# The chunk of the maximum pass ahead of the scores, in TensorE's queue and in the ring of PSUM banks

## The chip, the cores and the metric

The kernel runs on one core of one Trainium2 chip. The metric is the time of one execution in microseconds (us) of device time. Engines: TensorE multiplies matrices (PE in the profile, PEld for its weight loads), VectorE is DVE, ScalarE is ACT, GpSimd is POOL, SyncE is SP and issues DMAs.

## The reference

A block with cross attention and a mixture of experts, float32, for a batch of 4, 256 queries and 1601 keys, model width 128, 16 heads of 8:

```python
x = x + tanh(g_xattn[0]) * xattn(layernorm(x), ctx, ctx, mask, W_Q, W_K, W_V, W_T)
x = x + tanh(g_ffn[0]) * ffn(layernorm(x), w1, w2, router_w)
# xattn: heads of 8 columns
score = einsum('bhqd,bhkd->bhqk', Q, K) / sqrt(8)
score = where(mask == 0, -1e9, score)
out = einsum('bhqk,bhkd->bhqd', softmax(score), V) @ W_T
# ffn: 8 experts of 256, the two best by router
h = einsum('td,eid->tei', x, w1)
y = h[..., 256:] * silu(h[..., :256])
out = einsum('tei,ehi,te->th', y, w2, combine)
```

## The kernel before

The work is cut into 16 units, one for each of 4 batches and 4 groups of 4 heads; unit u is group u % 4 of batch u // 4. For an exact softmax each row of scores needs its maximum first. So TensorE computes the scores twice: once with queries in the rows, in chunks of up to 512 keys, of which VectorE takes the maximum (the maximum pass, 26 chunks a unit, `chunk`, L1013 and L757), and once with keys in the rows (`scores`, L1031), where the negated maximum is already in, as three more rows of the queries. ScalarE takes the exponential of these (`exponentials`, L622), and TensorE multiplies them by the values (`probs_v`, L1064).

A unit has 26 slots. In each slot stands one scores item, two key tiles of 128 keys for one head, a bank full; and one chunk. The chunks run 12 slots ahead of the scores (`LEAD`), so most are of the next unit; in the first 24 slots of unit 0 every even slot has two, until the lead is reached. `chunks_in(n)` lists the chunks of slot n. There are none after slot 13 of unit 14. A chunk of 512 keys is one matmul; chunks 12 and 25 of a unit hold the last 65 keys of four heads, in four short matmuls.

Both kinds of item go through one ring of five PSUM banks. `ring_tables` (L132) deals the banks out in the order of TensorE's queue, and notes for each item which item had its bank before; `ring_free` (L1008) makes TensorE wait until that one has been read, by ScalarE (`probs_ready`) for scores or by VectorE (`chunk_used`) for a chunk.

All engines run through the units and slots in the same written order, each with its own queue. After scores and chunk, a slot can have on TensorE:

- a piece of the key or value projection for a later batch (`piece`, L1050), in units 0 to 3;
- values times exponentials: four key tiles at once in slots 9, 17 and 25 (32 matmuls with those of two passes), the last short tile in slot 2 of the next unit;
- the transposes of the finished heads (slot 8) and of the negated maxima of the next unit (slot 17, L953; slot 20 in unit 0);
- in the first unit of each batch from the second on, for the batch before: slot 12 transposes the heads, slot 14 projects them (L1125), slot 20 transposes the normalised rows (L1131), slot 22 computes the router (L1136);
- in the other three units of such a batch, for the batch before: a tile of an expert's first layer every 4 or 5 slots (`expert_up`, L1100; slots 3, 8, 12, 16, 21, 25 of unit 6), and an expert's second layer six slots after its second tile (`expert_down`, L1108; slots 5, 14, 22 of unit 6).

VectorE's queue has in each slot the chunk's maximum (L767) first, then what the slot has for it: the gating of a tile (L853, L857), which waits for ScalarE's tanh (L659) of that tile; the add of an expert (L865); in a first unit the residual and statistics (slot 14, L797 to L804), the norm (slot 18, L811), the two best experts (slot 22, L819 to L828); in a second unit the routing weights (slot 1, L834 to L843). ScalarE's queue has the exponential first, then the rest.

At slot 0 of a unit the scores wait for the negated maxima's rows (`neg_in`), which a DMA has brought. The first chunk of a unit waits for that unit's keys and queries (`ld_unit`). Unit 0 starts 43.5 us after the span's start, unit 2 at 99.5, unit 4 at 149.3, unit 5 at 170.4, unit 6 at 198.8, unit 7 at 225.4, unit 8 at 250.4, unit 14 at 401.0 and unit 15 at 422.8 us.

Of the kernel before, what the change touches and what calls it, by code (L numbers as in the profile page):

```python
# [101 lines left out]
def following(b, q, by=1):  # L102

    return (b + (q + by) // NQ, (q + by) % NQ)


def chunk_rows(n):

    t, r = divmod(n, QH * (CH - 1) + 1)
    if r < QH * (CH - 1):  # L110
        return t, [r % QH], r // QH
    return t, list(range(QH)), CH - 1


def chunk_at(g):

    return 1 + g // CHUNKS, g % CHUNKS


def chunks_in(n):  # L120

    first = n + min(LEAD, (n + 1) // 2)
    last = n + 1 + min(LEAD, (n + 2) // 2)
    return [g for g in range(first, last) if g < CHUNKS * (B * NQ - 1)]


def neg_slot(u, s):

    return s + (FIRST_LATER if u == 0 else 0)


def ring_tables():  # L132

    banks, before = {}, {}
    latest = {i: ("quad", len(QUADS)) for i in range(RING)}
    item = 0
    for n in range(B * NQ * SLOTS):
        for kind, m in [("scores", n)] + [("chunk", g) for g in chunks_in(n)]:
            bank = item % RING
            banks[kind, m] = bank  # L140
            before[kind, m] = latest[bank]
            latest[bank] = (kind, m + 1)
            item = item + 1
    return banks, before


def piece_at(slot):

    u, s = divmod(slot, SLOTS)
    if s not in PIECE_SLOTS or u < 0:  # L150
        return None
    n = u * len(PIECE_SLOTS) + PIECE_SLOTS.index(s)
    return n if n < len(PIECES) else None
# [12 lines left out]
def expert_work(b, q, s, after=0):  # L166

    return [n for n, at in enumerate(TILE_AT[b - 1]) if at + after == (q - 1) * SLOTS + s]
# [7 lines left out]
def value_tiles(s):  # L176

    at = [VISIT // 2 * QH * (t // VISIT + 1) + 1 for t in range(KT - 1)] + [SLOTS + 2]
    return [(at[t] // SLOTS, t) for t in range(KT) if at[t] % SLOTS == s]


def block_kernel(nc, x, ctxT, mask, g_x, g_f, W_Q, W_K, W_V, W_T, w1T, w2T, rT, out):
# [5 lines left out]
    with es:  # L188
# [81 lines left out]
        ring, pv_bank, up_bank, down_bank = bank[0:RING], bank[5], bank[6], bank[7]  # L270
        down_b = down_bank.bitcast(BF16)
        ring_bank, ring_before = ring_tables()


# [645 lines left out]
        def _(pe):  # L920
# [84 lines left out]
            def attention(with_mask):  # L1005


                def ring_free(kind, n):  # L1008

                    earlier, count = ring_before[kind, n]  # L1010
                    pe.wait_ge({"scores": probs_ready, "chunk": chunk_used, "quad": quad_used}[earlier], count)

                def chunk(g):  # L1013

                    u, n = chunk_at(g)
                    q = u % NQ
                    if n == 0:
                        pe.wait_ge(ld_unit[q], 16 * (PARTS + 1) * (u // NQ + 1))

                    t, heads_in, c = chunk_rows(n)  # L1020
                    dst = ring[ring_bank["chunk", g]]
                    ring_free("chunk", g)
                    for i, j in enumerate(heads_in):
                        last = nc.tensor.matmul(dst[:, i * CW[c]:(i + 1) * CW[c]], queries[q][0:ROWS, j, t * P:(t + 1) * P],  # L1024
                                                keys[q][0:ROWS, j, c * BANK:c * BANK + CW[c]], start=True, stop=not with_mask)
                        if with_mask:
                            last = nc.tensor.matmul(dst[:, i * CW[c]:(i + 1) * CW[c]], ident_neg[:, :],
                                                    masked_q[:, t, c * BANK:c * BANK + CW[c]], start=False, stop=True)
                    last.then_inc(chunk_ready, 1)

                def scores(b, q, s):  # L1031

                    if s == 0:
                        pe.wait_ge(neg_in, 16 * PARTS * (NQ * b + q + 1))
                    n = SLOTS * (NQ * b + q) + s
                    slot_bank = ring[ring_bank["scores", n]]
                    ring_free("scores", n)
                    for i in range(2):
                        j, t = (s % QH, 2 * (s // QH) + i) if s < QH * (STEPS - 1) else (2 * (s % QH) + i, KT - 1)
                        w = P if t < KT - 1 else TAIL  # L1040
                        dst = slot_bank[0:w, i * S:(i + 1) * S]
                        last = nc.tensor.matmul(dst, keys[q][0:KR, j, t * P:t * P + w], queries[q][0:KR, j, :],  # L1042
                                                start=True, stop=not with_mask)
                        if with_mask:
                            for half in range(QT):
                                last = nc.tensor.matmul(dst[:, half * P:(half + 1) * P], masked_q[:, half, t * P:t * P + w],
                                                        ident_neg[:, :], start=False, stop=half == QT - 1)
                    last.then_inc(scores_ready, 1)

                def piece(n):  # L1050

                    kind, b, i = PIECES[n]
                    hold(pe, piece_out, n)
                    if b and (n == 0 or PIECES[n - 1][1] != b):
                        pe.wait_ge(ld_ctx[b], 16)
                    if kind == "Q":
                        cols = slice(S + i * BANK, min(S + (i + 1) * BANK, B * S))
                        made = nc.tensor.matmul(up_bank[:, 0:cols.stop - cols.start], wq[:, :], xnT[:, cols],
                                                start=True, stop=True)
                    else:  # L1060
                        made = project_keys(b, i, up_bank) if kind == "K" else project_values(b, i, up_bank)
                    made.then_inc(piece_ready, 1)
# [85 lines left out]
                def units(b, tail, attn, last):  # L1148
                    for q in range(NQ):
                        u = NQ * b + q  # L1150
                        for s in range(SLOTS):
                            before = not (q == 0 and not tail) and (attn or q == 0)
                            if attn:
                                scores(b, q, s)
                                for g in chunks_in(SLOTS * u + s):
                                    chunk(g)
                                if piece_at(SLOTS * u + s) is not None:
                                    piece(piece_at(SLOTS * u + s))
                            for back, kt in value_tiles(s):
                                if before if back else attn:  # L1160
                                    probs_v(u - back, (q - back) % NQ, kt)
                            if s == S_OTR and before:
                                pe.wait_ge(out_copied, u)
                                down_bank_free(b, tail, q, s, attn, last)
                                for t in range(QT):
                                    tr = nc.tensor.transpose(down_bank[:, t * P:(t + 1) * P],
                                                             head_outT[:, t * P:(t + 1) * P], ident[:, :])
                                tr.then_inc(out_T, 1)
                            if s == neg_slot(u, S_MTR) and attn and not (last and q == NQ - 1):
                                down_bank_free(b, tail, q, s, attn, last)  # L1170
                                neg_transpose(*following(b, q))
                            if tail and q == 0:
                                if s in (S_PROJ, S_ROUTE):
                                    down_bank_free(b, tail, q, s, attn, last)
                                tail_slot(b, s)
                            for n in expert_work(b, q, s) if tail and attn else ():
                                expert_up(b, n, [up_bank])
                            for n in expert_work(b, q, s, DOWN_AFTER) if tail and attn else ():
                                if n % TILES == TILES - 1:
                                    down_bank_free(b, tail, q, s, attn, last)  # L1180
                                    expert_down(b, n // TILES, down_bank)
                            if q == 0 and not attn:
                                fill_slot(b, s)
# [62 lines left out]
```

## Time and profile before

| what | value |
|---|---|
| time, median of 3 runs | 481.47 us (477.12 to 485.35) |
| profiled execution: its own time | 480.24 us |
| profiled execution: span | 478.4 us |
| granted TensorE clock, mean | 0.978 |
| TensorE busy | 444.4 us, 93% |
| VectorE busy | 350.6 us, 73% |
| ScalarE busy | 273.9 us, 57% |
| GpSimd busy | 85.9 us, 18% |

The span goes from the first to the last instruction; the execution's time has some 2 us around it. Busy times are of one execution. The ends of matmuls are modelled, and neighbouring ones overlap in the rows, so the distance of two starts tells more than a duration.

### The profile page before, as it was taken

How to read it: one execution, taken by the hardware profiler on the slowest of the kernel's cores; microseconds unless marked ns; L12 is line 12 of the kernel's file. 1: busy time of each engine (PE TensorE's matmuls, PEld its weight loads, DVE VectorE, ACT ScalarE, POOL GpSimd, SP SyncE). 2: the span in 40 equal slices, each digit the busy share in tenths (PEclk: the TensorE clock that was granted, in tenths of full speed). 3: DMA queues.
4: the chain of work that ended last, by engine and by line, in shares of the span. 5: the costliest groups of instructions: out<-in, count | busy, mean ns of one | idle time of the engine just before them, and what ended most of it. 6: DMA issues, size and time to landing. Idle time of an engine off the chain costs nothing.

```text
span 478.4 us, 10091 instructions
## 1 busy us (share of the span) xinstructions
PE 444.4 (93%) x3864; PEld 266.6 (56%) x3866; DVE 350.6 (73%) x768; ACT 273.9 (57%) x569; POOL 85.9 (18%) x207
## 2 busy tenths in 40 slices
PE   7873999998999999999999999999999989999896
PEld 3331555644554556666665556666655456566786
DVE  3971786764768897887888987888879777531786
ACT  4201666764768665665657665665667565687221
POOL 4800508236820100000001100000001000000000
PEclk9995999999999999999999999999999898999999
DMA  7476626693734040404014403012052200000000
GB/s 271 99 166 170 141 79 159 185 241 107 194 106 103 5 87 0 91 3 87 6 35 80 88 6 78 14 43 50 2 113 46 46 2 1 2 13 1 1 11 12
DMA packets 20701, 35.23 MB, mean 74 GB/s; under 512 B 2236, under 2 KB 12924, under 8 KB 20524
## 3 DMA queue, kind: packets, MB, share of 16 engines
q1 hardware_dynamic: 19348, 33.96, 29.5%
q10 hardware_dynamic: 1304, 0.59, 0.5%
q8 instruction: 33, 0.54, 0.5%
q14 instruction: 16, 0.13, 0.1%
HBM read 26.49 MB, written 7.80 MB: 72 GB/s over the span
## 4 chain that ended last, share of the span: by engine, by line
PE 69%; DVE 14%; ACT 5%; DMA 4%; issue 4%; POOL 2%; SPq 0%; POOLq 0%; DVEq 0%; ACTq 0%
PE banks L1076 19%; PE banks L1042 16%; PE banks L1024 13%; PE banks L1100 10%; PE banks L1108 5%; DVE chunk_max L767 5%; DMA queries<-neg_rows 3%; DVE chunk_max L749 3%; ACT probs L636 3%; PE banks L931 2%; DVE late L853 2%; PE banks L925 1%; DVE late L857 1%; DMA probs<-x 1%; ACT late L659 1%
## 5 line engine op out<-in xcount | busy, mean ns | idle before, releaser
L767 DVE TENSOR_REDUCE chunk_max<-banks 128x1 f32<-128x512 f32 (+1 forms) x390 | 240.0, 663 | 67.4 <-PE banks L1024 66.6
L636 ACT ACTIVATE probs<-banks 128x512 f32<-128x512 f32 x384 | 210.8, 605 | 94.6 <-PE banks L1042 93.7
L1042 PE MATMUL banks<-queries,keys 75*128 75x256 bf16 (+1 forms) x832 | 157.0, 276 | 13.9 <-DMA queries<-neg_rows 9.2
L1024 PE MATMUL banks<-keys,queries 72*128 72x512 bf16 x480 | 146.7, 339 | 2.2 <-DVE chunk_max L767 0.9
L1042 PEld LDWEIGHTS banks<-queries,keys 75*128 75x128 bf16 (+1 forms) x832 | 72.0, 100 | 82.9 <-DVE chunk_max L767 28.9
L1076 PE MATMUL banks<-probs,value_t 128*9 128x256 f32 x1536 | 93.6, 384 | 0.1
L1076 PEld LDWEIGHTS banks<-probs,value_t 128*9 128x9 f32 x1536 | 37.4, 91 | 46.3 <-issue 12.1
L1024 PEld LDWEIGHTS banks<-keys,queries 72*128 72x128 bf16 x480 | 42.3, 97 | 22.5 <-ACT probs L636 7.6
L659 ACT ACTIVATE late<-banks 128x256 f32<-128x256 f32 x64 | 24.6, 385 | 49.6 <-PE banks L1100 44.1
L853 DVE SCALAR_TENSOR_TENSOR late<-late,banks 128x256 f32<-128x256 f32 x64 | 26.7, 417 | 30.1 <-ACT late L659 30.0
L1100 PE MATMUL banks<-xn2T,w 128*128 128x256 f32 x128 | 35.4, 400 | 1.3 <-DVE late L857 1.3
L1108 PE MATMUL banks<-w,late 128*128 128x128 f32 x256 | 34.0, 276 | 1.2 <-DVE late L857 1.0
L1108 PEld LDWEIGHTS banks<-w,late 128*128 128x128 f32 x256 | 33.1, 191 | 3.1 <-DVE x L865 1.2
L1100 PE MATMUL banks<-late,w 128*128 128x256 f32 x128 | 32.0, 381 | 0.0
L469 POOL COPY value_t<-values 128x384 f32<-128x384 f32 x16 | 8.0, 503 | 130.7 <-PE banks L1076 127.7
L530 POOL TENSOR_SCALAR neg_max<-row_max 128x8 f32<-128x8 f32 x16 | 3.8, 236 | 145.2 <-DVE row_max L744 145.2
L857 DVE TENSOR_TENSOR late<-late,banks 128x256 f32<-128x256 f32 x64 | 26.9, 421 | 2.2
L1100 PEld LDWEIGHTS banks<-xn2T,w 128*128 128x128 f32 x128 | 24.1, 199 | 6.2 <-DVE late L857 2.1
L865 DVE SCALAR_TENSOR_TENSOR x<-banks,combine,x 128x128 f32<-128x128 f32 x64 | 19.3, 343 | 8.8 <-PE banks L1108 8.7
L1100 PEld LDWEIGHTS banks<-late,w 128*128 128x128 f32 x128 | 23.2, 190 | 3.7 <-issue 0.9
L645 ACT COPY neg_rows<-banks 12x256 bf16<-12x256 bf16 x16 | 5.8, 360 | 27.8 <-PE banks L953 27.8
L639 ACT ACTIVATE probs_tail<-banks 65x512 f32<-65x512 f32 x32 | 17.6, 591 | 1.6 <-PE banks L1042 1.6
(121 smaller groups left out, 288.2 us busy)
## 6 DMA issues: line engine op xcount, KB each, us to landing
keys<-k_parts SPq DMA_DIRECT2D x48, 300.2 KB
k_parts<-split SPq DMA_DIRECT2D x6, 400.2 KB, 7.6
ctx_in<-ctxT SPq DMA_DIRECT2D x3, 800.5 KB, 5.2
k_parts<-late SPq DMA_DIRECT2D x6, 400.2 KB, 4.8
queries<-q_parts SPq DMA_DIRECT2D x16, 144.0 KB
w<-w1T SPq DMA_DIRECT2D x1, 2048.0 KB, 14.8
q_parts<-q_split SPq DMA_DIRECT2D x9, 192.0 KB, 2.6
w<-mask SPq DMA_DIRECT2D x2, 800.5 KB, 6.6
```

The source lines that it names most:

```text
L636: nc.scalar.activation(probs[:, s % (HELD * QH), :], ring[ring_bank["scores", n]][:, :], ACT.Exp, scale=SCALE).then_inc(probs_ready, 1)
L639: nc.scalar.activation(probs_tail[0:TAIL, s % QH, :], ring[ring_bank["scores", n]][0:TAIL, :], ACT.Exp, scale=SCALE).then_inc(probs_ready, 1)
L659: nc.scalar.activation(th[:, n % 2, :], bank[:, 0:S], ACT.Tanh, scale=0.5).then_inc(th_ready, 1)
L767: nc.vector.reduce_max(dst, src, axis=AX.X).then_inc(chunk_used, 1)
L853: steps.link(nc.vector.scalar_tensor_tensor(gated[:, :], th[:, n % 2, :], 1.0, bank[:, 0:S], ALU.add, ALU.mult))
L857: nc.vector.tensor_tensor(inner[:, n % 4, :], gated[:, :], bank[:, S:2 * S], ALU.mult).then_inc(inner_ready, 1)
L865: last = nc.vector.scalar_tensor_tensor(x1[:, t, :], bank[:, t * D:(t + 1) * D], combine[:, t, e:e + 1], x1[:, t, :], ALU.mult, ALU.add)
L1024: last = nc.tensor.matmul(dst[:, i * CW[c]:(i + 1) * CW[c]], queries[q][0:ROWS, j, t * P:(t + 1) * P], keys[q][0:ROWS, j, c * BANK:c * BAN ...
L1042: last = nc.tensor.matmul(dst, keys[q][0:KR, j, t * P:t * P + w], queries[q][0:KR, j, :], start=True, stop=not with_mask)
L1076: last = nc.tensor.matmul(pv_bank[32 * j:32 * j + HW, 0:S], value_t[q % 2][0:w, kt, j, :], p, start=kt == 0, stop=kt == KT - 1)
L1100: last = nc.tensor.matmul(banks[n % len(banks)][:, k * S:(k + 1) * S], w1[:, e, k * INTER + i * P:k * INTER + (i + 1) * P], xn2Ts[b % 2][: ...
L1108: last = nc.tensor.matmul(bank[:, t * D:(t + 1) * D], inner[:, (TILES * e + i) % 4, t * P:(t + 1) * P], w2[:, e, i, :], start=i == 0, stop ...
```

## The change

In the loop of TensorE's queue the call of `scores` moves from ahead of the slot's chunks to behind them. `ring_tables` gives out the banks in the same new order. VectorE's, ScalarE's and the other queues stay as they are.

```diff
--- before.py
+++ after.py
@@ -135,7 +135,7 @@
     latest = {i: ("quad", len(QUADS)) for i in range(RING)}
     item = 0
     for n in range(B * NQ * SLOTS):
-        for kind, m in [("scores", n)] + [("chunk", g) for g in chunks_in(n)]:
+        for kind, m in [("chunk", g) for g in chunks_in(n)] + [("scores", n)]:
             bank = item % RING
             banks[kind, m] = bank
             before[kind, m] = latest[bank]
@@ -1151,9 +1151,9 @@
                         for s in range(SLOTS):
                             before = not (q == 0 and not tail) and (attn or q == 0)
                             if attn:
-                                scores(b, q, s)
                                 for g in chunks_in(SLOTS * u + s):
                                     chunk(g)
+                                scores(b, q, s)
                                 if piece_at(SLOTS * u + s) is not None:
                                     piece(piece_at(SLOTS * u + s))
                             for back, kt in value_tiles(s):
```

## Rows read from the trace of the kernel before

**Rows 1.** The page: TensorE's busy time; the chain's shares by engine.

```profile
PE 444.4 (93%) x3864; PEld 266.6 (56%) x3866; DVE 350.6 (73%) x768; ACT 273.9 (57%) x569; POOL 85.9 (18%) x207
...
PE 69%; DVE 14%; ACT 5%; DMA 4%; issue 4%; POOL 2%; SPq 0%; POOLq 0%; DVEq 0%; ACTq 0%
```

**Rows 2.** Windows: units 4 and 6; length, each engine's busy us, clock.

```profile
149.30:170.40 21.10, 20.26 (x208) 11.34 (x204) 18.20 (x45) 14.74 (x30) 2.63 (x9) 1.00 0.30 58
198.80:225.40 26.60, 26.49 (x242) 17.23 (x240) 22.16 (x47) 16.25 (x34) 1.67 (x7) 1.00 0.21 43
```

**Rows 3.** Waits: who waited for whom, us in all, times, longest.

```profile
PEld banks L1042 <- DVE chunk_max L767: 28.9, 78, 1.2
...
PE banks L1042 <- DMA queries<-neg_rows: 9.2, 2, 8.2
...
PEld banks L1024 <- ACT probs L636: 7.6, 29, 0.6
```

**Rows 4.** Groups by form: busy us and mean ns of one.

```profile
L767 DVE TENSOR_REDUCE chunk_max<-banks 128x1 f32<-128x512 f32 x360 | 228.3, 683 | 56.0 <-PE banks L1024 55.3 <-DVE combine L843 0.3
L636 ACT ACTIVATE probs<-banks 128x512 f32<-128x512 f32 x384 | 210.8, 605 | 94.6 <-PE banks L1042 93.7
```

**Rows 5.** The chain, slots 0 to 9 of unit 7: start, us, what.

```profile
225.64 0.22 PE banks L1042 x2
225.86 0.12 PE banks L1024 x4
...
226.99 0.55 PE banks L1076 x8
...
228.09 0.86 PE banks L1100 x4
...
229.61 0.22 PE banks L1024
229.83 0.89 PE banks L1108 x8
...
233.53 0.22 PE banks L1042 x2
...
233.97 1.84 PE banks L1076 x32
```

**Rows 6.** Timeline, unit 7: start, us, engine, line, count of merged instructions.

```profile
226.89 2.21 DVE L767 TENSOR_REDUCE chunk_max<-banks 128x4 f32<-128x260 f32 x4
227.48 0.39 PE L1042 MATMUL banks<-queries,keys 75*128 75x256 bf16 x2
230.20 1.28 DVE L767 TENSOR_REDUCE chunk_max<-banks 128x1 f32<-128x512 f32 x2
231.54 0.28 PE L1042 MATMUL banks<-queries,keys 75*128 75x256 bf16 x1
...
231.91 1.88 DVE L767 TENSOR_REDUCE chunk_max<-banks 128x1 f32<-128x512 f32 x3
...
235.97 0.38 PE L1024 MATMUL banks<-keys,queries 72*128 72x512 bf16 x1
...
236.39 0.69 DVE L767 TENSOR_REDUCE chunk_max<-banks 128x1 f32<-128x512 f32 x1 [0.85 <-PE banks L1024]
```

**Rows 7.** Timeline, slots 17 and 25 of unit 4, and VectorE there.

```profile
161.28 0.38 PE L1042 MATMUL banks<-queries,keys 75*128 75x256 bf16 x2
...
161.81 0.66 DVE L767 TENSOR_REDUCE chunk_max<-banks 128x1 f32<-128x512 f32 x1
...
168.05 0.40 PE L1042 MATMUL banks<-queries,keys 75*65 75x256 bf16 x2
...
169.09 3.05 DVE L767 TENSOR_REDUCE chunk_max<-banks 128x1 f32<-128x512 f32 x5
```

**Rows 8.** Windows: 3.4 us of unit 5, and the 3.4 us after them.

```profile
173.80:177.20 3.40, 2.59 (x15) 1.00 (x14) 3.37 (x7) 2.57 (x5) 0.00 (x0) 1.00 0.11 20
177.20:180.60 3.40, 3.40 (x12) 2.08 (x9) 2.05 (x6) 1.21 (x3) 0.00 (x0) 0.50 0.02 5
```

## The prediction, as it was made before the result

> **What bounds the kernel now.** I read first which engine is full, then by units what is full where, then whose waits are met, and only then single instructions. The page gives TensorE 93% of the span, and the chain of waits puts 69% of it on TensorE and 14% on VectorE [rows 1]. By stretches, the units with expert work (unit 6, 26.6 us) have TensorE busy 26.49 us, so nearly every us added to its queue is a us of the span; VectorE is busy 22.16 us there, 83%. In unit 4 (a first unit of a batch) TensorE has 20.26 of 21.10 us [rows 2]. TensorE is the bound from unit 4 on, with VectorE close behind. In the list of waits TensorE's weight loads wait 28.9 us for VectorE's maxima in front of scores and 7.6 us for ScalarE's exponentials in front of chunks [rows 3]. Most of this is covered, since loads run ahead of matmuls: the chain through unit 7 is TensorE alone, 28 of its 29 pieces, of which rows 5 has the eight that I use [rows 5]. So ring waits cost almost nothing now, though many are nearly due. The question is which of them come due earlier.
>
> **The change, part by part.** No instruction is added or removed; every slot still has one scores item, its chunks and then its rest (value tiles, an expert tile, a transpose). What moves:
>
> 1. *The banks.* Five banks go round, scores and chunks in turn. Before, item 2n is the scores of slot n, and the item five back is the chunk of slot n-3; the chunk's is the scores of slot n-2. After, the scores need the bank of the chunk of slot **n-2**, and the chunk that of the scores of slot **n-3**. TensorE may enter the rest of a slot before with three chunks unread by VectorE and two scores unread by ScalarE, afterwards with two chunks and three scores. The buffer is moved from the slower reader to the faster one: a chunk takes VectorE 683 ns, a scores tile takes ScalarE 605 ns, and VectorE alone also has the gating and adding for the experts [rows 4]. Unit 0, where even slots have two chunks, is different: five items to two slots, each bank is taken again by its own kind two slots later in both orders, so nothing changes there.
>
> 2. *The queue.* The chunk goes 0.22 us earlier and the scores 0.22 us later (length of one chunk, 0.12 for the one of four short matmuls) [rows 5]. TensorE's total is the same, so this alone costs zero. At a unit's first slot the chunk passes the wait for the row of negated maxima; the list has 9.2 us of that in two places [rows 3], which a chunk can't shorten; it fills 0.22 us of it each time, and a little of VectorE's work. I take -0.4 us for both. A chunk that waited for keys would now hold the scores behind it; no row shows TensorE waiting for keys, so zero.
>
> 3. *Waits on ScalarE.* At least one slot more lies between exponential and chunk. That can save what now stands on ScalarE, between 0 and the 7.6 us of weight load waits [rows 3]. I count it where it shows: the places of before that I subtract below hold those waits, the places of after don't.
>
> 4. *Waits on VectorE.* This is the term that decides, and I work it out slot by slot for unit 7 with rows' durations. Scores 0.22, chunk 0.22 (0.12 in slots 0 and 13), short value tile 0.55, expert tile up 0.86, down 0.89, visit to the values 1.84 [rows 5]. VectorE starts a chunk 0.42 after its matmul starts (235.97 to 236.39), needs 0.68, back to back 0.59 to 0.60 each (five in 3.05 [rows 7]), and the bank can be written 0.06 after the end (two chunks from 230.20 on end at 231.48, the scores start at 231.54). After an expert tile the next chunk starts 1.41 after the tile's last matmul (225.48 to 226.89), since VectorE's in-order queue waits at the gate for ScalarE's tanh; an add of an expert costs it 0.51 (the second of those two chunks starts at 230.80, the next at 231.91; less 0.60) [rows 6].
>
> Clock zero at 225.48, the end of the tile at the previous slot 25. Chunk 0 starts at 0, scores 0 at 0.12, chunk 1 at 0.35, scores 1 at 0.57, chunk 2 at 0.79, scores 2 would start at 1.01. It needs chunk 0, which VectorE reads from 1.41 to 1.83: **wait of 0.88**. In the order before, it is the scores of slot 3 that need chunk 0, and they start at 227.48, 0.16 us after that read's end [rows 6]. Then the short value tile, chunk 3 and scores 3 (2.99), the tile up to 4.08. Chunks 4 and 5, down, chunk 6: scores 6 wait 0.15 for chunk 4, scores 7 wait 0.16 for chunk 5, scores 8 wait 0.67 for chunk 6, which stands behind the add. The tile of slot 8 ends at 9.54; before, this was 7.89 (from 225.64 to 233.53 on the chain [rows 5]). **Slots 0 to 9: +1.65.** In slots 10 to 17 scores 12 wait 0.05 and scores 16 wait 0.37 (chunk 14 behind the gate): **+0.44**. In slots 18 to 25 of unit 6, scores 20, 21 and 24 wait 0.05, 0.16 and 0.16, and scores 25 wait 0.67 for chunk 23, which stands behind an add: with what was waited there before taken off, **+0.97**; in unit 7, with no tile at 21, +0.5.
>
> First units of a batch (4, 8, 12) have no expert tiles, but three VectorE jobs that wait for TensorE. Slots 3 to 9: +0.16. Scores of slot 17 need chunk 15, which stands behind the residual and is read from 161.81 to 162.47, where TensorE was at slot 17 at 161.28: with the short delays before it (0.39 at the projection, whose exponentials come 0.22 later) +1.44. Scores of slot 25 need chunk 23, behind the top-2 search and read from 169.09 to 169.77, where TensorE was at 168.05 [rows 7]: with the scores' own place 0.22 later and the norm's 0.22 earlier, +1.57. About **+3.1** a unit. Second units (5, 9, 13): scores 4 need chunk 2 behind the routing weights, a little over 1 us, but there TensorE waited before too: +0.8 in slots 0 to 9.
>
> Sum: slots 0 to 9 of units 6, 7, 10, 11, 4 x 1.65 = 6.6; slots 10 to 17 of six units, 2.6; slots 18 to 25, 4 x 0.97 + 2 x 0.5 = 4.9; first units 3 x 3.1 = 9.3; second units 3 x 0.8 = 2.4; the rest of 13 and 14, where tiles are rarer and which I only estimate, 1.5; units 1 to 3, where the same working gives gains at ScalarE waits (slots 5 to 9 of unit 2, -0.2) and losses of the same size, 0; unit starts -0.4. Together **+26.9 us**. From unit 14's middle on there are no chunks, so nothing. Ends of this term: if readers catch up in ways that the working misses, half of it, +13; if every unit from 1 to 14 lost the 3.1 of the dearest kind, +43.
>
> 5. *TensorE's clock.* In one stretch of 3.4 us in unit 5 the granted clock is 0.50, that is 1.2 instead of 2.4 GHz, and in the 3.4 us before it TensorE was busy for 2.59 us only [rows 8]; two more stretches like it are in unit 13. Each costs half its length, 1.7 us. The same pattern in unit 9 passed without it, so it isn't certain. The new waits of 0.65 us or more make some 24 such stretches (waits as in slots 2, 8, 25, 17) where there were some seven, of which three were throttled. At that rate seven more; since several have less idle time than the old ones I take three more, **+5 us**; ends 0 and 24 x 1.7 = 41.
>
> The Trainium skill ("TensorE: Matmul & The Clock Gate", "A second HAM failure mode: psum-queue depth-cycling") says that short idle times between matmul groups which cycle through PSUM banks can make the clock swing between its two rates. The trace before shows three swings and agrees as far as it goes; taken fully the rule gives the first rival below, by which the sum would be nearer its upper end.
>
> Profiled execution 480.24 us (span 478.4, 1.8 us around it) + 26.9 + 5 = 512.1; it lies 1.2 us under the median of 481.47, so I say **512 us**.
>
> **The rivals.**
> *The clock swings all through*: mechanism of step 5 at its upper end. For it: three of the seven idle stretches of before were followed by it; against: the other four. 480 + 27 + 30 to 41 us = 537 to 548.
> *VectorE catches up*: it has 17% free in unit 6, and a wait of TensorE gives it time. If a delayed scores item only moves idle time that now comes later at the values' visit, the loss is a few us: 480 + 5 = 485. Against: TensorE has no idle time in unit 6 to give back (26.49 of 26.6).
> *Faster*: ScalarE's waits go (7.6 us of loads [rows 3]) and the chunk passes the wait for the negated maxima. Place: units 1 to 3, which have no expert work, and the starts of units 0 and 2. At best 7.6 + 2 x 0.7 (a chunk less to read after the wait) = 9 us: 471. It decides if chunk n-2 is read by the time scores n come, that is if VectorE's backlog stays under two chunks; the gate rows say that it doesn't.
> That the change doesn't act is excluded by the bank table.
>
> **How the numbers follow.** Forecast 0.76 (its own range 496 to 530); clock rival 0.08; catching up 0.12; faster 0.04. No change means within 2%, 9.6 us, about what this kernel's measurements (477.12 to 485.35) can tell. Faster by over 2% is half of the last case, 0.02; within 2% is the other half, and catching up, 0.14; slower 0.84. The range reaches to the lower end of the clock rival and, at the bottom, to half of step 4's sum: 494 to 538; outside are the two lowest cases, 0.16, and some of the clock rival.
>
> **What would show it.** In the changed profile: scores matmuls idle before them on chunk_max, tens of us in place of a few, with waits of 0.7 to 1.1 us in slots 2, 8 and 25; chunks no longer waiting for ScalarE; unit 6 at 29.7 us and unit 4 at 24.2 us; units 0 to 3 within 0.5 us each; from slot 14 of unit 14 the same length; more clock rows at 0.50. The forecast is wrong if VectorE's waits at gates shrink because the tiles move against its queue, which my working holds fixed at 1.41 us.

## The result, and the profile after

The changed kernel takes 511.18 us (median of 4 executions, 504.75 to 520.44) beside 479.64 us before (477.12 to 485.35): a ratio of 1.065 with a 95% interval of 1.059 to 1.072, slower. Forecast were 512 us and a range of 494 to 538. An execution's time moves with its mean granted clock: of the four of the changed kernel the shortest had 0.978, the longest 0.949. The profiled execution took 510.16 us, its span is 508.4 us.

Of the page: TensorE's busy line, the granted clock in 40 slices, the chain's shares, and the group of the scores matmuls (busy us, mean ns | idle time before them, and what ended it).

```profile
PE 459.7 (90%) x3864; PEld 259.5 (51%) x3866; DVE 352.4 (69%) x768; ACT 284.2 (56%) x569; POOL 86.0 (17%) x207
...
PEclk9995699999999989999999999999999799999999
...
PE 60%; DVE 20%; ACT 6%; issue 5%; DMA 4%; POOL 3%; ACTq 1%; SPq 0%; POOLq 0%; DVEq 0%
...
L1042 PE MATMUL banks<-queries,keys 75*128 75x256 bf16 (+1 forms) x832 | 160.9, 280 | 22.1 <-DVE chunk_max L767 21.8
```

Against [rows 1] the instructions are the same in number, and VectorE's work has hardly grown, yet its share of the chain went from 14% to 20% and TensorE's from 69% to 60%. The list of waits (us in all, times, longest) has the place, and answers to [rows 3]:

```profile
PEld banks L1042 <- DVE chunk_max L767: 69.1, 141, 1.5
...
PE banks L1042 <- DVE chunk_max L767: 21.8, 36, 1.1
...
PE banks L1024 <- DMA queries<-q_parts: 7.7, 1, 7.7
...
PEld banks L1024 <- ACT probs L636: 5.8, 17, 0.4
```

Weight loads of scores wait 69.1 us for VectorE's maxima instead of 28.9, and the matmuls themselves 21.8 us in 36 places. The same row for the matmuls in the kernel before:

```profile
PE banks L1042 <- DVE chunk_max L767: 4.3, 7, 0.8
```

Slots 0 to 9 of unit 7 in the changed kernel, the stretch that the prediction replayed, in the timeline of TensorE (start, us, engine, line; a scores item is one row of two matmuls):

```profile
238.41 0.28 PE L1024 MATMUL banks<-keys,queries 72*128 72x65 bf16 x4
...
239.19 0.38 PE L1024 MATMUL banks<-keys,queries 72*128 72x512 bf16 x1
240.30 0.39 PE L1042 MATMUL banks<-queries,keys 75*128 75x256 bf16 x2 [0.73 <-DVE chunk_max L767]
240.62 0.62 PE L1076 MATMUL banks<-probs_tail,value_t 65*9 65x256 f32 x8
241.18 0.39 PE L1024 MATMUL banks<-keys,queries 72*128 72x512 bf16 x1
...
244.26 0.38 PE L1024 MATMUL banks<-keys,queries 72*128 72x512 bf16 x1
244.64 0.39 PE L1042 MATMUL banks<-queries,keys 75*128 75x256 bf16 x2
...
245.24 0.39 PE L1042 MATMUL banks<-queries,keys 75*128 75x256 bf16 x2
245.47 0.38 PE L1024 MATMUL banks<-keys,queries 72*128 72x512 bf16 x1
246.35 0.39 PE L1042 MATMUL banks<-queries,keys 75*128 75x256 bf16 x2 [0.50 <-DVE chunk_max L767]
246.58 0.40 PE L1166 MATMUL banks<-ident,head_outT 128*128 128x128 f32 x2
246.81 1.03 PE L1100 MATMUL banks<-xn2T,w 128*128 128x256 f32 x4
247.68 0.38 PE L1024 MATMUL banks<-keys,queries 72*128 72x512 bf16 x1
```

And VectorE there (the row at 239.82 is three chunks merged, of which chunk 0 is the first):

```profile
239.03 0.42 DVE L853 SCALAR_TENSOR_TENSOR late<-late,banks 128x256 f32<-128x256 f32 x1 [2.63 <-ACT late L659]
239.48 0.42 DVE L857 TENSOR_TENSOR late<-late,banks 128x256 f32<-128x256 f32 x1
239.82 1.61 DVE L767 TENSOR_REDUCE chunk_max<-banks 128x4 f32<-128x260 f32 x3
...
245.10 0.60 DVE L865 SCALAR_TENSOR_TENSOR x<-banks,combine,x 128x128 f32<-128x128 f32 x2
```

With clock zero at 238.41, the scores of slot 2 start at 1.89; they could have at 1.00 (239.19 and 0.22). What they wait for is chunk 0, at the head of VectorE's row at 239.82 and behind the two gating instructions; ahead of the first VectorE sat idle for 2.63 us until tanh came. Scores 6, 7 and 8 start at 6.23, 6.83 and 7.94, the last 0.66 late behind the add at 245.10. The waits of the prediction, added up from the same zero, put them at 1.89, 6.23, 6.83 and 7.94.

In the chain of the changed kernel, answering to [rows 5], what was TensorE alone is now a relay of ScalarE, VectorE and TensorE:

```profile
238.61 0.39 ACT late L659
...
239.03 0.43 DVE late L853
...
239.48 0.42 DVE late L857
239.90 0.35 DVE chunk_max L767
240.25 0.05 issue
240.30 0.39 PE banks L1042 x2
```

The lengths of the units (start of a unit's first scores to the next unit's, from the timeline), before, after, and in a second profile of the changed kernel (run e12 below), with what was forecast:

| unit | before | after | again | difference, e12 to before | forecast |
|---|---|---|---|---|---|
| 0 | 30.47 | 34.74 | 30.34 | -0.1 | within 0.5 |
| 4 | 21.15 | 25.21 | 25.46 | 4.3 | 3.1 |
| 6 | 26.61 | 29.46 | 29.47 | 2.9 | 3.1 |
| 7 | 24.94 | 27.40 | 27.40 | 2.5 | 2.6 |
| 8 | 21.16 | 23.83 | 23.83 | 2.7 | 3.1 |
| 9 | 26.74 | 28.92 | 28.94 | 2.2 | 2.2 |
| 12 | 21.16 | 25.07 | 23.84 | 2.7 | 3.1 |
| 4 to 14 | 273.47 | 298.86 | 298.65 | 25.2 | 27.3 |

Unit 4 holds a stretch of 3.4 us with the clock at 0.50 in both profiles of the changed kernel and none in that of before; without it its loss is that of unit 8. Over units 4 to 14 the profile of before and that of e12 have three such stretches each, so the 25.2 us are nearly all the banks'.

### The profile page after: what moved, and what is told of

Its sections match the earlier page's. It is cut to its first block, busy times and chain, and to the rows that moved or that the text cites. A ratio compares the mean times of both kernels' runs of the same rounds, so it can differ in the third digit from the quotient of the medians.

```text
span 508.4 us, 10091 instructions
## 1 busy us (share of the span) xinstructions
PE 459.7 (90%) x3864; PEld 259.5 (51%) x3866; DVE 352.4 (69%) x768; ACT 284.2 (56%) x569; POOL 86.0 (17%) x207
## 4 chain that ended last, share of the span: by engine, by line
PE 60%; DVE 20%; ACT 6%; issue 5%; DMA 4%; POOL 3%; ACTq 1%; SPq 0%; POOLq 0%; DVEq 0%
PE banks L1076 19%; PE banks L1042 14%; DVE chunk_max L767 10%; PE banks L1024 10%; PE banks L1100 9%; DVE late L853 3%; ACT late L659 2%; PE banks L1108 2%; ACT probs L636 2%; PE banks L925 2%; DMA queries<-q_parts 2%; PE banks L931 2%; DVE x L865 2%; DVE late L857 2%; ACTq L608 1%
## 5 line engine op out<-in xcount | busy, mean ns | idle before, releaser
L636 ACT ACTIVATE probs<-banks 128x512 f32<-128x512 f32 x384 | 215.4, 604 | 118.7 <-PE banks L1042 116.7
L1042 PE MATMUL banks<-queries,keys 75*128 75x256 bf16 (+1 forms) x832 | 160.9, 280 | 22.1 <-DVE chunk_max L767 21.8
L1024 PE MATMUL banks<-keys,queries 72*128 72x512 bf16 x480 | 149.5, 346 | 8.6 <-DMA queries<-q_parts 7.7
L1042 PEld LDWEIGHTS banks<-queries,keys 75*128 75x128 bf16 (+1 forms) x832 | 70.8, 101 | 108.5 <-DVE chunk_max L767 69.1
L1076 PE MATMUL banks<-probs,value_t 128*9 128x256 f32 x1536 | 95.8, 390 | 0.1
L853 DVE SCALAR_TENSOR_TENSOR late<-late,banks 128x256 f32<-128x256 f32 x64 | 26.8, 418 | 43.9 <-ACT late L659 43.5
L1108 PEld LDWEIGHTS banks<-w,late 128*128 128x128 f32 x256 | 31.6, 191 | 2.7 <-DVE x L865 1.2
L857 DVE TENSOR_TENSOR late<-late,banks 128x256 f32<-128x256 f32 x64 | 26.9, 420 | 2.2
L1100 PEld LDWEIGHTS banks<-xn2T,w 128*128 128x128 f32 x128 | 22.7, 197 | 5.7 <-DVE late L857 2.1
L639 ACT ACTIVATE probs_tail<-banks 65x512 f32<-65x512 f32 x32 | 18.8, 594 | 7.5 <-PE banks L1042 7.3
```

The costliest lines, as they stand in the source:

```text
L636: nc.scalar.activation(probs[:, s % (HELD * QH), :], ring[ring_bank["scores", n]][:, :], ACT.Exp, scale=SCALE).then_inc(probs_ready, 1)
L639: nc.scalar.activation(probs_tail[0:TAIL, s % QH, :], ring[ring_bank["scores", n]][0:TAIL, :], ACT.Exp, scale=SCALE).then_inc(probs_ready, 1)
L853: steps.link(nc.vector.scalar_tensor_tensor(gated[:, :], th[:, n % 2, :], 1.0, bank[:, 0:S], ALU.add, ALU.mult))
L857: nc.vector.tensor_tensor(inner[:, n % 4, :], gated[:, :], bank[:, S:2 * S], ALU.mult).then_inc(inner_ready, 1)
L1076: last = nc.tensor.matmul(pv_bank[32 * j:32 * j + HW, 0:S], value_t[q % 2][0:w, kt, j, :], p, start=kt == 0, stop=kt == KT - 1)
L1100: last = nc.tensor.matmul(banks[n % len(banks)][:, k * S:(k + 1) * S], w1[:, e, k * INTER + i * P:k * INTER + (i + 1) * P], xn2Ts[b % 2][: ...
```

## The experiments

All run beside the kernel before on the same chip: its median was 481.33 us beside e1 to e4, 483.58 beside e5 to e8 and 478.75 beside e9 to e12. An execution's clock moves its time by up to 4%, so for differences smaller than that the units' lengths decide, which agree to 0.02 us between two profiles of one kernel except where the clock was at 0.50.

**Where the loss lies: units from 4 on, units to 3 (e4, e5).** The new order in both places, for part of the slots (`ring_tables` has the same condition, not shown here):

```diff
+scores_first = not ((SLOTS * u + s) >= 4 * SLOTS)      # e5: not (... < 4 * SLOTS)
+if scores_first:
+    scores(b, q, s)
 for g in chunks_in(SLOTS * u + s):
     chunk(g)
-scores(b, q, s)
+if not scores_first:
+    scores(b, q, s)
```

> The change from unit 4 on only; units 0 to 3 as before. Theory: units 4 to 14 carry the whole of it, +25 us without clock stretches: 503 to 512 us, unit 6 at 29.5 us, units 0 to 3 at their old lengths. Rival (unit 0's +4.2 us in the changed kernel belongs to the new order there, through the clock): this one is 4 us faster than the changed kernel, and its unit 0 has the clock at 0.50 for 10 us after 37 us, not 20.

> The change in units 0 to 3 only. Theory: 480 us, the same as before within 3; unit 0's +4.2 us in the changed kernel came from TensorE's clock, which stayed at 0.50 for 20 us after 39.6 us there by the chance of one execution. Rival (the new order at the start of unit 0 keeps the clock low): +4 us and again some 20 us at 0.50.

e4: 513.2 us (505.56 to 519.75), ratio 1.064 (1.047 to 1.081), 1 us over the 503 to 512 expected; units 6 and 7 at 29.47 and 27.40 us, as in the changed kernel. e5: 481.96 us beside 483.58, units 4 to 12 as before within 0.01 us but for unit 5, which escaped a clock stretch (26.74 for 28.41). So units 4 to 14 carry all of it, within what the clock lets be seen. Unit 0 with the new order took 30.42 us in e5: its 34.74 us in the changed kernel's first profile isn't the order's. There the clock was at 0.50 for 20.5 us from 39.6 on, in e5 for 10.2 us from 38.3 on.

**Once more the same (e12).** No edit.

> The changed kernel once more, for what varies between executions. Theory: the waits on VectorE are the same to 0.1 us in each unit (unit 6 29.5, unit 7 27.4 us), the stretches with the clock at 0.50 lie elsewhere and unit 0's is 10 us long in most executions; 503 to 513 us. Rival: unit 0 has 20 us at 0.50 again.

505.58 us (505.12 to 506.77), ratio 1.058 (1.051 to 1.064). Unit lengths as in the table: only units with a clock stretch in one of the two profiles, or in both, differ. The 10 us in unit 0 came as expected.

**The two halves of the diff (e1, e2).** e1 has only the edit in TensorE's queue, e2 only the one in `ring_tables`.

> The queue of the change with the banks of before: TensorE issues chunk, then scores, but the scores of slot n still take the bank of chunk n-3 and the chunk that of scores n-2. Theory (VectorE lost one of its three unread chunks ahead of a slot's rest): nothing is lost, 480 us, give or take 4; unit 6 stays at 26.6 us. Rival (the place in the queue costs: exponentials come 0.22 us later, so tanh and gates come later): most of the +31 us stays, 505 to 515 us.

> The banks of the change with the queue of before: TensorE issues scores, then chunk, and the scores of slot n take the bank of chunk n-2. Theory: all the loss is there and more, since the scores reach that wait one chunk (0.22 us) earlier and hold the slot's own chunk behind them: 515 to 540 us. Rival (queue order): 480 us.

e1: 503.28 us (496.02 to 515.89), ratio 1.045 (1.031 to 1.058). Unit 6 took 28.16 us, unit 4 23.60. The theory was wrong, and the rival's number (505 to 515) nearly met, but the waits of e1 say something that neither had:

```profile
PEld banks L1024 <- ACT probs L636: 53.4, 128, 0.6
...
PE banks L1024 <- ACT probs L636: 20.1, 83, 0.4
...
PEld banks L1042 <- DVE chunk_max L767: 4.8, 15, 0.4
```

VectorE is waited for by almost nothing, as the theory has it, but chunks wait for ScalarE 83 times. With the banks of before and the queue of the change a chunk is only three items behind the scores whose bank it takes, 0.66 us in slots without a rest, and a scores item needs over 1 us from its start to the end of its exponential, here from 213.97 to 214.99 (timeline of e1):

```profile
213.97 0.38 PE L1042 MATMUL banks<-queries,keys 75*128 75x256 bf16 x2
...
214.39 0.60 ACT L636 ACTIVATE probs<-banks 128x512 f32<-128x512 f32 x1
```

e2 is the mirror (`PEld banks L1042` waits for VectorE again, here in e2): 548.92 us (543.53 to 553.28), ratio 1.141 (1.128 to 1.154), unit 6 at 31.22 us; scores are three items behind the chunk whose bank they take, and wait 97 times for VectorE:

```profile
PEld banks L1042 <- DVE chunk_max L767: 108.1, 170, 1.7
PE banks L1042 <- DVE chunk_max L767: 44.9, 97, 1.3
```

So the halves aren't the change in two parts: each alone shortens one distance in TensorE's queue from five items to three, and lengthens the other to seven. The loss by the theory is there in e2, and larger than expected (515 to 540). In its profile the clock was at 0.50 for 30.7 us behind unit 0, against 10.2 us before; by half of the difference that is an estimated 10 us of time, about the excess over 540.

**The order of banks kept, the rest moved (e3).** Queue and banks of the change, but the rest of a slot comes between chunk and scores; ScalarE takes the exponential behind its own rest, so tanh isn't held up (that edit isn't shown here):

```diff
 for g in chunks_in(SLOTS * u + s):
     chunk(g)
-scores(b, q, s)
 ...
 if q == 0 and not attn:
     fill_slot(b, s)
+if attn:
+    scores(b, q, s)
```

> Queue and banks of the change, but TensorE does the rest of a slot (value tiles, expert tiles, transposes) between its chunk and its scores, and ScalarE takes the exponential after its own rest of the slot. The order of all banks is that of the change, scores n behind chunk n-2. Theory: what counts is how many chunks are unread when the rest begins, and that is three again: 480 us, up to 486. Rival (a scores item that needs chunk n-2 is late wherever it stands): 505 to 515 us.

482.46 us (478.06 to 491.00), ratio 1.005 (0.997 to 1.012): no difference from before. Unit 6, as a window (length, then busy us of TensorE, its weight loads, VectorE, ScalarE, GpSimd), beside [rows 2]:

```profile
195.10:221.70 26.60, 26.50 (x244) 17.23 (x240) 22.17 (x48) 16.23 (x34) 1.68 (x7) 1.00 0.22 45
```

The scores still take chunk n-2's bank, and come even later; the whole loss is gone. Weight loads of scores wait 31.4 us for VectorE, about the 28.9 of before. It isn't the bank that scores n take and not their later place that costs, but that the wait stands ahead of the rest, so that VectorE has two unread chunks instead of three when TensorE turns to it. Seen from the queue this is no wonder: scores, next chunk, rest is the pattern of the kernel before, with the scores of one slot earlier in it. The edit to ScalarE's queue came with it and wasn't tested alone.

**No common ring (e10, e11).** e10 has the queue of the change with three banks for chunks and two for scores, e11 the queue of before with two and three.

```diff
-            bank = item % RING
+            bank = m % 3 if kind == "chunk" else 3 + m % 2    # e10
+            bank = m % 2 if kind == "chunk" else 2 + m % 3    # e11
```

> The change's queue, but no common ring: three banks for chunks, two for scores. A chunk needs chunk n-3 (six items back), scores need scores n-2 (four items back, 0.88 us in slots without a rest, where ScalarE needs 1.08 from the start of a scores item to its bank being free). Theory: waits on VectorE all but go, waits of some 0.2 us on ScalarE come in runs of bare slots: unit 6 at 27.0 to 27.8 us, 486 to 494 us in all. Rival (the place in the queue costs): 505 us or more.

> The queue of before, scores then chunk, with two banks for chunks and three for scores: chunk n needs chunk n-2, four items back, ahead of the slot's rest. Nothing of the new queue order is left, only the smaller buffer of VectorE. Theory: slower than the changed kernel, since each wait on VectorE comes one item earlier: unit 6 at 29.8 to 31 us, 515 to 535 us. Rival (the new order in the queue is needed for the loss): 480 to 485 us.

e10: 496.35 us (495.39 to 498.55), ratio 1.039 (1.032 to 1.045), 2 us over what was expected; unit 6 at 27.28 us, inside it. Its loss is mostly not where the change has its own. Of the 16.5 us between the spans of the two profiles units 4 to 13 have 4.8 (with two clock stretches for three), units 1 to 3 have 2.1, and units 14 and 15 have 3.7 (a clock stretch in it) and 5.2 (none in it). There are no chunks from the middle of unit 14 on, and the scores are left with two banks out of five: 4.3 of the 5.5 us that scores matmuls wait for ScalarE in e10 stand there, from 421 us on. The expectation left that out. e11: 524.69 us (523.38 to 527.38), ratio 1.098 (1.091 to 1.105), unit 6 at 29.89 us, all as expected. e11 has nothing of the new order but the smaller buffer for VectorE, and unit 6 loses more than in the change (29.47). Of its 46 us an estimated 12 are the clock's, by half of the difference of 34.1 and 10.2 us at 0.50 behind unit 0. Its wait is at the chunk, which needs the bank of chunk n-2:

```profile
PE banks L1024 <- DVE chunk_max L767: 24.5, 45, 1.3
```

e10's waits are on the other side:

```profile
PEld banks L1042 <- ACT probs L636: 53.6, 133, 0.8
PEld banks L1024 <- DVE chunk_max L767: 23.0, 62, 1.1
...
PE banks L1042 <- ACT probs L636: 5.5, 17, 0.5
```

Together with e1: with the queue order of the change the place of the wait follows from the distances in the ring, not from the order.

**A faster VectorE (e6, e7).** The maximum of a 512 key chunk over its first 256 keys alone (the other half of each row is left out, so the row maxima are partial), in the kernel before (e6) and in the changed one (e7).

```diff
-src[:, 0:CW[c]]
+src[:, 0:CW[c] // 2]
```

> The kernel before, with the maximum of a 512 key chunk taken over its first 256 keys only (left out: half of VectorE's reads, so the row maxima are partial). A base for the next one. Some us faster than before at most, since TensorE is the bound: 470 to 481 us.

> The changed kernel with the same half maxima. Theory: the waits behind a plain backlog of chunks go, those behind a VectorE job that itself waits (the gate of slot 25's tile, the residual, the router's top-2, the routing weights) stay, since chunk n-2 stands behind it however short it is: 8 to 14 us more than the kernel before with half maxima. Rival 1 (only VectorE's throughput counts): no difference, under 3 us. Rival 2 (place in the queue): the full 30 us.

467.11 us (464.33 to 469.75) and 486.79 us (483.59 to 491.24), so 19.7 us apart, more than the 8 to 14 expected. The second profile has the long clock stretch in unit 0, which makes 5.1 us of the 18.9 between the spans. Without unit 0 the two differ by 1.4 us in unit 6, 1.1 in units 7 and 9 and 1.5 in unit 4, 13.4 us over units 4 to 14, against some 25 of the full reads. That is inside the 8 to 14 us, and the slots bear out the split (starts of scores, e7 against e6, and in brackets e12 against before). At the places that step 4 of the prediction puts behind a VectorE job with a long wait of its own, most of the loss stays: the distance from the scores of the slot before grows at slot 2 of unit 6 (gate) by 0.89 us (0.89), at slot 17 of unit 8 (residual) by 0.76 (1.02), at its slot 25 (two best experts) by 0.75 (1.23). At the others less stays: at slots 8, 16 and 25 of unit 6 0.19 (0.58), 0.11 (0.37) and 0.30 (0.68). e6 was 3 us faster than its expectation; in units 5 and 13 the waits of scores matmuls for VectorE are half as long (0.4 for 0.8 us and 1.2 for 2.4), and no clock stretch is left.

**The gate behind the next chunk (e8, e9).** VectorE does the gating of a tile and the add of an expert a slot later, behind the next chunk; e8 is the changed kernel, e9 the one before.

```diff
+for f, *what in held:      # behind the slot's chunk
+    f(*what)
+held.clear()
 ...                        # later in the same slot
-gate_tile(b, n, up_bank)
+held.append((gate_tile, b, n, up_bank))
 ...                        # the add of an expert likewise
```

> The changed kernel, but VectorE does the gating of a tile and the add of an expert one slot later, behind the next slot's chunk. Theory: chunk 0 is then read before the gate that waits for tanh, so the wait at slot 2 goes, and those behind gates and adds shrink; units 5 to 7 and 9 to 11 lose 0.5 us each instead of 1.8 to 2.9, first units keep their 2.7 us: 491 to 499 us in all. Rival (the lost buffer costs wherever VectorE has work, whatever stands in front): 505 us or more.

> The kernel before, with the gating of a tile and the add of an expert one slot later in VectorE's queue. Could be a version better than both. Theory: TensorE is the bound and doesn't wait behind gates now, so within 2 us, 478 to 482; the few waits at VectorE in units 5, 9 and 13 may go, and with them a clock stretch or two, 476. Rival (tanh and gate later mean the expert's second layer waits): slower by a few us.

e8: 503.95 us (498.44 to 510.18), ratio 1.054 (1.015 to 1.093), above the 491 to 499 expected; as a whole time it doesn't tell this kernel from the changed one. Its profiled execution took 498.44 us. The units go the way of the theory: unit 6 at 27.47 us, so 0.9 lost instead of 2.9, where 0.5 was expected. The first slots of unit 7 (lines are numbered four higher than before for TensorE, one for VectorE's gate):

```profile
229.60 0.28 PE L1028 MATMUL banks<-keys,queries 72*128 72x65 bf16 x4
...
229.93 0.43 DVE L767 TENSOR_REDUCE chunk_max<-banks 128x4 f32<-128x260 f32 x1 [1.82 <-PE banks L1028]
...
230.27 0.41 DVE L854 SCALAR_TENSOR_TENSOR late<-late,banks 128x256 f32<-128x256 f32 x1
...
230.60 0.38 PE L1046 MATMUL banks<-queries,keys 75*128 75x256 bf16 x2
```

Chunk 0 is read ahead of the gate, and the scores of slot 2 start 1.00 us after chunk 0 (229.60), without a wait. A part of what the units gained the clock took: behind unit 0 this profile has six stretches of 3.4 us at 0.50, the one of before three, so by half of the difference an estimated 5 us.

e9: 478.69 us (475.88 to 483.79), ratio 0.9995 (0.994 to 1.005). Units 5, 9 and 13 gain (26.17, 26.17 and 26.67 us for 28.41, 26.74 and 29.97), in units 5 and 13 mostly the clock stretches that are gone; units 6, 7, 10 and 11 lose 0.62 each in slots 3 to 9. It doesn't beat the kernel before.

## Why the prediction was right

*Steps 1 and 4, the banks: right, shown.* e3 and e11 take the two readings apart. With the scores behind their chunk, but three unread chunks at the start of the rest, nothing is lost; with the queue of before and two unread chunks 46 us are, clock included. Measured by slots, with the forecast in brackets (differences of before and after in the timeline, from scores to scores): slots 0 to 9 of unit 7 +1.48 (1.65), slots 10 to 17 +0.47 (0.44), slots 18 to 25 of unit 6 +0.91 (0.97), of unit 7 +0.51 (0.5). From chunk 0 to chunk 9 of unit 7 the prediction has 9.54 us and the trace 9.27 (238.41 to 247.68). The 0.27 too many came from the rest of slot 8: it took 1.38 us before, in which an issue gap stood, and 1.10 after (246.58 to 247.68). Two waits of a first unit (unit 4), timeline of the changed kernel:

```profile
166.51 1.85 DVE L767 TENSOR_REDUCE chunk_max<-banks 128x1 f32<-128x512 f32 x3
...
167.23 0.39 PE L1042 MATMUL banks<-queries,keys 75*128 75x256 bf16 x2 [0.86 <-DVE chunk_max L767]
...
173.02 0.38 PE L1024 MATMUL banks<-keys,queries 72*128 72x512 bf16 x1
...
174.59 1.89 DVE L767 TENSOR_REDUCE chunk_max<-banks 128x1 f32<-128x512 f32 x3
...
175.34 0.41 PE L1042 MATMUL banks<-queries,keys 75*65 75x256 bf16 x2 [1.06 <-DVE chunk_max L767]
```

Both waits are where [rows 7] let them be expected, at slots 17 and 25. In units without clock stretches slots 10 to 17 lost 1.27 (1.44) and slots 18 to 25 1.24 (1.57): a fifth too much. From the router's matmuls (their end is the next chunk's start, 173.02) to chunk 23's read at 174.59 it took 1.57 us, where I had taken the 1.9 us of before, in which VectorE still had chunk 22 to read first. For slots 10 to 17 the cause of the difference is open.

The whole of step 4 was +26.9, of it +27.3 in units 4 to 14. Measured there, with three clock stretches on either side: +25.2, 2 us less.

*Step 5, the clock: the mechanism is seen in unit 4, the +5 us are not.* Windows in unit 4 of the changed kernel:

```profile
172.70:176.10 3.40, 2.34 (x22) 1.29 (x25) 3.26 (x14) 2.09 (x5) 0.00 (x0) 1.00 0.72 150
176.10:179.50 3.40, 3.40 (x35) 1.44 (x28) 0.60 (x2) 0.28 (x1) 0.00 (x0) 0.50 0.78 146
```

After the wait at 175.34 (TensorE busy 2.34 of 3.4 us) the clock fell to 0.50, 1.2 GHz, and the visit to the values took 3.23 us instead of 1.91: the same sequence as [rows 8]. It came in unit 4 in both profiles of the changed kernel and in those of e4 and e8, in unit 12 in one of the changed kernel's, in unit 8 in neither; in unit 4 of before and of e5 there is none. Behind unit 0 the first profile has four such stretches and the second three, as that of before had; the fourth is worth 1.7 us, and the long one of unit 0 another 4.3 (34.74 for 30.42), 6.0 us together. The prediction counted 24 candidates and three more stretches than before; the profiles have one more and none more, and candidates like slot 2's were followed by none. Most of the clock's 6.0 us in the first profile stands in unit 0, where the prediction has no term, and where the order isn't its cause (10.2 us at 0.50 in e5 and e12 with the new order, 23.9 in e9 with the old). So it is luck that 512 and 511.18 lie 1 us apart: step 4 was 2 us too high, and step 5's sum was met by another stretch than the ones it counted. In e12 the kernel takes 505.58 us, 26.8 above the one before beside it, and the clock adds next to nothing; the forecast's range holds this too. Between executions of the changed kernel time goes with the clock: 504.75 us at a mean of 0.978, 520.44 at 0.949. The rule of the Trainium skill ("TensorE: Matmul & The Clock Gate", "A second HAM failure mode: psum-queue depth-cycling") that short idle times between matmul groups which cycle through PSUM banks can make the clock swing agrees with the rows of unit 4, and not with the many idle times that no swing followed. In e2 and e8 the stretches beyond those of before cost an estimated 10 and 5 us. The rival that it swings all through didn't come about.

*Step 2, the queue: right in the sum, one sentence wrong.* It said that no chunk waits for keys. After the change the first chunk waits 7.7 us for unit 1's queries, at the place where scores waited for the negated maxima. It cost next to nothing: the first chunk started at 43.10 us, where in the profile of before the scores waited for the negated maxima until 43.48; behind their two chunks the scores then started at 43.91, without a wait.

*Step 3, ScalarE's waits: right that it is small.* Weight loads of chunks still wait 5.8 us for it, for 7.6; the forecast that this would vanish was wrong. Where those left stand is open.

*The rival "VectorE catches up"* is refuted by units of 29.46 for 26.61 us, the faster one by units 1 to 3, which e5 shows at the old time.

What stays open: why the clock stretch at the start of unit 0 lasts 10 us in most profiles and 20 to 24 in four of fourteen, e9 with the old order among them.

## What to carry to other kernels

With a ring of buffers shared by two readers, look at what stands between taking a buffer and the next long job of the producer: the number of unread buffers of each kind at that moment is the real depth for each reader. Exchange two items and the depth goes from one reader to the other; give it to the one whose queue has jobs that wait. And a bank table and the order of the queue are one thing: either changed alone shortened a distance from five items to three, and lost 22 us (the queue) and 68 us (the banks), clock included. Separate rings need a look at the parts in which one kind is missing: in e10 the scores lost 5.2 us in the last unit, beside three banks that nobody used.

## What the runs showed of the hardware that wasn't expected

TensorE kept busy doesn't mean a raised clock at once: in the first profile of the changed kernel its rows (whose ends are modelled) fill the time from 43.9 to 60.06 us without a gap, and the clock stayed at 0.50 until then. Two of the windows there:

```profile
43.90:47.30 3.40, 3.40 (x9) 1.46 (x8) 1.80 (x3) 1.20 (x2) 0.00 (x0) 0.50 0.90 297
...
54.10:57.50 3.40, 3.40 (x19) 2.61 (x17) 2.33 (x4) 2.09 (x5) 2.13 (x4) 0.50 0.00 0
```

In the profile of before the clock rose at 47.5, after 4 us of such work. And a kernel with fewer waits can have more clock stretches: e8's units are shorter than the changed kernel's where no stretch falls in them, and its profile has six stretches behind unit 0 for three and four.
